# A graph-network and feed-forward kernel on one core: finer waits in the edge trees, roots issued sooner, group 0's rows merged tile by tile, and the sums of chunks 38, 40 and 42 moved to TensorE

## The chip, the cores and the metric

The kernel is one program on one core of a Trainium2 chip. A core has TensorE (PE, matrix products into PSUM), VectorE (DVE), ScalarE (ACT), GpSimd (POOL) and SyncE (SP), each with its own queue of instructions, and 16 DMA engines that all queues share. Engines wait for each other through semaphores. The metric is the device time of one execution in microseconds (us); 0.2% of it is 2.4 us.

## The reference

6250 nodes with 256 features, 200,000 edges with 96 features, sorted by destination `dst`. What the change touches is the first part of the layer:

```python
xn = layernorm(x)
out1 = segment_sum(edge_attr, dst, 6250)
cnt  = segment_sum(1, dst, 6250)
out2 = where(cnt > 0, segment_max(edge_attr, dst, 6250), 0)
out3 = out1 / maximum(cnt, 1)
h    = concat([xn, out1, out2, out3, u])
gnn  = relu(h @ W1 + b1) @ W2 + b2 + xn
mix  = linear_attention(xn)      # q, k squared and normalised, kv, projection
x    = x + gnn + mix
x    = x + ffn(layernorm(x))     # on the half of the nodes with the largest weights
```

## The kernel before

**Edges.** The edges are padded and laid out as 128 partitions of 1568 rows, in 49 chunks of 32 rows per partition. A chunk (1536 KB) is loaded into one of four buffers `xb` by a DMA on SP's queue. Four consecutive rows form a quad, so a chunk has 8 quads. On DVE (`edge_chunk`) a tree first reduces each quad: L995 and L999 take maxima, L998 and L1002 take sums. Then a scan over the 8 quads runs with one step for the maximum (L1018) and one for the sum (L1021) per quad, each from the step before, and writes `ob` (two buffers). SP stores `ob` to `scan_d` in DRAM (a dump, L575), then loads the chunk that is four ahead (L577). Before its first scan step a chunk waits for the dump of the chunk two before it, since it reuses that buffer. For the chunks in `SUMS` the sums of quads come from TensorE instead (`quad_sums`, L1943): four products with the identity for each half chunk, accumulated in one PSUM bank; DVE leaves L998 and L1002 out and its steps L1021 read PSUM. These are chunks 1, 2 and 44 to 48.

**Nodes beside them.** While DVE works through the chunks, TensorE and ScalarE make the projections of 13 groups of 512 nodes (`turn`), with a small normalisation of the keys by DVE after fixed chunks (`NORM`); DVE's key norms of the last two groups come behind chunks 32 and 33. After chunk 35 DVE makes factors (`s_fac`), ScalarE scales the matrix `M` (L1703), and TensorE runs `attention` for the groups (L2122), with ScalarE evicting (L1744), storing each group and fetching the one four ahead on its own DMA queue. In between, the weights of the network are loaded by SP (L596, L599), copied by ScalarE (h0 to h5, L1717) and their low parts made (l0 to l11, L2093) at the groups that `WORK` lists. After chunk 39 DVE computes which rows each node gathers (`rows_to_gather`, ends `s_idx`), after chunk 41 their masks.

**End of the edges.** POOL gathers the raw edge rows of group 0 (`raw0`), ScalarE masks them (L1773 after chunk 46, L1779 after chunk 47). When chunk 48 is done, SP dumps it, and POOL gathers group 0's scan rows (L500), the row to be repaired (L710), group 1's raw rows, writes the repaired row back, gathers group 1's scan rows, then all rows of group 2, and then adds the attention rows to the base rows of group 0 (L756, `bg`). DVE merges group 0's rows for all four tiles at once (`aggregate`, parts 2 to 4) into `agg`; TensorE transposes `agg` (L2168) and begins the hidden layer. The second product of the network (L70, L71) writes PSUM banks psR and psC, and DVE adds `bg` to them (L1182) before the next tile's product may overwrite the bank.

**The rest.** The network over 49 node tiles, the selection of 3124 nodes and the last network follow, with TensorE in the lead.

Of the kernel before, what the change touches and what calls it, by code (L numbers as in the profile page):

```python
# [18 lines left out]
GT = 4  # L19
# [54 lines left out]
def build(nc, x, dstp, edges, u, W1, b1, W2, b2, Wqkv, bqkv, Wout, bout, wr, br, w1, fb1, w2, fb2, out):  # L74
# [10 lines left out]
    with keep:  # L85
# [33 lines left out]
        with ExitStack() as ctx:  # L119
# [331 lines left out]
            psS = {c: psKx if c in SUMS_EARLY else [psR, psC] for c in SUMS}  # L451
# [5 lines left out]
            def weight_piece(i):  # L457
                if i < 8:
# [5 lines left out]
            WORK = {4: ("h0",), 5: ("h1", "l0", "l1"), 6: ("h2", "l2", "l3"), 7: ("h3", "l4", "l5"), 8: ("h4", "l6", "l7"),  # L464
                    9: ("h5", "l8", "l9"), 10: ("l10", "l11")}
# [85 lines left out]
            def _(sp):  # L551
# [18 lines left out]

                def dump_and_load(c, b, load):
# [16 lines left out]
                for c in range(36, CHUNKS):  # L588
# [5 lines left out]
                    if c in (36, 37, 38):  # L594
                        for i in ((0, 1), (2,), (3,))[c - 36]:
                            sp.dma_start(rW1[:, i, :], W1[i * P:(i + 1) * P, :]).then_inc(s_wl[i], 16)  # L596
                    elif c in (39, 40):
# [1760 lines left out]
```

## Time and profile before

| what | value |
|---|---|
| median of 3 runs | 1180.55 us (1180.41 to 1182.44) |
| the profiled execution, its own time | 1180.66 us |
| its span | 1178.9 us |
| PE busy / DVE busy | 1051.5 us (89%) / 991.9 us (84%) |
| ACT busy / POOL busy | 500.4 us (42%) / 451.9 us (38%) |
| mean granted TensorE clock | 0.938 of full |

Busy times are sums over the whole span, which has several stages with different limits; a row of the timeline says what an engine waited for just before an instruction. "DMA share" is the mean busy share of the 16 DMA engines; it can read slightly over 1. A tile name loses its buffer number (`xb` for xb0 to xb3), and names of buffers that share memory are put down by one of them (`W1f_lo`, `rW`, `dprv` as the second query buffer).

### The profile page before, as it was taken

What the parts mean: (1) busy time and instruction counts of PE and PEld (TensorE: products, weight loads), DVE (VectorE), ACT (ScalarE), POOL (GpSimd) and SP (SyncE); (2) the same over time, 40 slices, a digit from 0 to 9 for tenths busy, and PEclk for the clock granted to TensorE, in tenths of its full rate; (3) what the DMA queues carried; (4) which work ended last, traced back from release to release, by engine and by line L of the source; (5) the groups of instructions that cost most, each with busy time, mean ns of one, the idle gap of its engine ahead of it and who ended that gap; (6) DMA issues with size and microseconds to landing.
All of it is one profiled execution on the core that took longest, in us unless ns stands there. A gap on an engine that the chain in (4) does not pass through costs nothing.

```text
span 1178.9 us, 16127 instructions
## 1 busy us (share of the span) xinstructions
PE 1051.5 (89%) x4683; PEld 781.9 (66%) x4683; DVE 991.9 (84%) x2410; ACT 500.4 (42%) x1487; POOL 451.9 (38%) x344
## 2 busy tenths in 40 slices
PE   2598999999988759888999999999999986799996
PEld 1355555656635536466888888888888972488886
DVE  7899999999999997966988889888897757576574
ACT  3547877778832422611332233322333323243341
POOL 0088810888300002076565445654443000223331
PEclk9798999999996979979999999999999996599998
DMA  9799999999988999533443333433333130111110
GB/s 344 288 318 371 346 376 365 356 376 360 335 315 330 415 418 366 189 120 90 133 148 127 123 102 126 150 124 125 107 102 123 54 108 17 38 37 42 46 43 20
DMA packets 76512, 234.99 MB, mean 199 GB/s; under 512 B 13105, under 2 KB 43094, under 8 KB 70178
## 3 DMA queue, kind: packets, MB, share of 16 engines
q1 hardware_dynamic: 42786, 157.00, 35.7%
q0 software_dynamic: 14224, 33.61, 10.0%
q10 hardware_dynamic: 19440, 43.66, 9.9%
q8 instruction: 26, 0.43, 0.2%
q14 instruction: 36, 0.29, 0.1%
HBM read 153.68 MB, written 80.55 MB: 199 GB/s over the span
## 4 chain that ended last, share of the span: by engine, by line
PE 49%; DVE 3%; POOL 2%; issue 1%; DMA 0%; ACT 0%; DVEq 0%; POOLq 0%
PE psR L70 5%; PE psC L70 5%; PE psQ L59 5%; PE psQ L60 5%; PE psKx L59 5%; PE psQ L61 5%; PE psKx L60 5%; PE psKx L61 5%; PE psR L71 3%; PE psC L71 2%; PE psT L2168 1%; PE psQ L2189 1%; PE psKx L2189 1%; POOL graw L474 1%; PE psR L69 1%
## 5 line engine op out<-in xcount | busy, mean ns | idle before, releaser
L474 POOL DMA_INDIRECT graw<-in_edge_attr,ic x90 | 128.7, 1430 | 33.1 <-issue 24.1
L1018 DVE SCALAR_TENSOR_TENSOR ob<-ob,mQ,mx 128x96 f32<-128x96 f32 x392 | 122.3, 312 | 13.4 <-PE psR L1943 6.5
L684 POOL DMA_INDIRECT near<-in_dst,rowi x49 | 87.8, 1792 | 63.8 <-DVEq L924 49.1
L1818 ACT ACTIVATE hT_hi<-psQ 128x512 fp32r<-128x512 f32 (+2 forms) x52 | 29.9, 575 | 186.0 <-PE psQ L2189 142.5
L684 POOL DMA_INDIRECT near<-ends_d,blki x49 | 82.3, 1679 | 68.0 <-DVEq L915 53.4
L1021 DVE SCALAR_TENSOR_TENSOR ob<-ob,kQ,xb 128x96 f32<-128x96 f32 x336 | 104.5, 311 | 0.0
L1970 PE MATMUL psQ<-Wqk,xT 128*128 128x512 f32 (+1 forms) x196 | 94.3, 604 | 0.0
L995 DVE TENSOR_TENSOR mx<-xb 128x1536 f32<-128x1536 f32 x49 | 85.6, 1747 | 1.2 <-DVE carry L1076 0.2
L998 DVE TENSOR_TENSOR xb<-xb 128x1536 f32<-128x1536 f32 x42 | 73.8, 1758 | 1.4
L500 POOL DMA_INDIRECT grow<-scan_d,ic x49 | 54.0, 1101 | 42.8 <-DMA scan_d<-ob 28.1
L70 PE MATMUL psR<-W2w,hT_hi 128*128 128x512 f32 x175 | 65.7, 411 | 3.9 <-DVE x L1184 3.9
L1818 ACT ACTIVATE hT_hi<-psKx 128x512 fp32r<-128x512 f32 (+2 forms) x52 | 29.8, 575 | 88.8 <-PE psKx L2189 88.7
L788 POOL DMA_INDIRECT out_x<-zo,lst x25 | 24.6, 986 | 104.7 <-DVE zo L1474 104.7
L70 PE MATMUL psC<-W2w,hT_hi 128*128 128x512 f32 x168 | 60.8, 399 | 0.0
L1991 PE MATMUL psKx<-xn,kc 128*128 128x257 f32 (+1 forms) x196 | 52.3, 390 | 5.2 <-ACT kc L1594 5.2
L480 POOL DMA_INDIRECT yg<-yrow_d,lst x25 | 24.9, 997 | 82.0 <-DVE lst L1426 74.7
L746 POOL COPY ic<-idx 128x12 int32 (+3 forms) x11 | 4.5, 407 | 134.5 <-PE psC L69 134.5
L1970 PEld LDWEIGHTS psQ<-Wqk,xT 128*128 128x128 f32 (+1 forms) x196 | 38.0, 194 | 26.9 <-issue 24.3
L1982 PE MATMUL psC<-WvoI,xT 128*128 128x256 f32 (+1 forms) x196 | 50.6, 381 | 0.0
L71 PE MATMUL psR<-W2w,hT_lo 128*128 128x256 f32 x175 | 49.9, 285 | 0.0
L71 PE MATMUL psC<-W2w,hT_lo 128*128 128x256 f32 x168 | 47.4, 282 | 0.0
L1174 DVE SCALAR_TENSOR_TENSOR hT_lo<-psQ,hT_hi 128x512 fp32r<-128x512 f32 (+2 forms) x52 | 34.0, 654 | 15.3 <-ACT hT_hi L1818 15.3
(533 smaller groups left out, 3284.4 us busy)
## 6 DMA issues: line engine op xcount, KB each, us to landing
xb<-in_edge_attr SPq DMA_DIRECT2D x49, 1536.0 KB
scan_d<-ob SPq DMA_DIRECT2D x49, 768.0 KB
yrow_d<-yr SPq DMA_DIRECT2D x48, 132.0 KB
xg<-in_x ACTq DMA_DIRECT2D x12, 512.0 KB
xT_d<-xT ACTq DMA_DIRECT2D x12, 512.0 KB
base_d<-dcur ACTq DMA_DIRECT2D x12, 512.0 KB
qT_d<-qT ACTq DMA_DIRECT2D x12, 512.0 KB
out_x<-xres SPq DMA_DIRECT2D x48, 128.0 KB
```

The costliest lines, as they stand in the source:

```text
L59: nc.tensor.matmul(out, lh, rh, start=start, stop=False)
L60: nc.tensor.matmul(out, lh, rl, start=False, stop=False)
L61: return nc.tensor.matmul(out, ll, rh, start=False, stop=stop)
L70: nc.tensor.matmul(out, lh, both.rearrange("p h n -> p (h n)"), start=start, stop=False)
L71: return nc.tensor.matmul(out[:, 0:NF], ll, both[:, 0, :], start=False, stop=False)
L474: nc.gpsimd.indirect_dma_start(out=to.rearrange("p i f -> p (i f)"), out_offset=None, in_=raw_v, in_offset=bass.IndirectOffsetOnAxis(ap=ic ...
L684: nc.gpsimd.indirect_dma_start(out=near[:, t, :], out_offset=None, in_=table, in_offset=bass.IndirectOffsetOnAxis(ap=rows[:, t:t + 1], axi ...
L995: nc.vector.tensor_tensor(mx[:, :, :, :], xp[:, :, :, 0, :], xp[:, :, :, 1, :], ALU.max).then_inc(s_tree, 1)
L998: nc.vector.tensor_tensor(xp[:, :, :, 0, :], xp[:, :, :, 0, :], xp[:, :, :, 1, :], ALU.add).then_inc(s_tree, 1)
L1018: nc.vector.scalar_tensor_tensor(o[:, q, 0:EF], prev[:, 0:EF], mQ[:, bass.ds(c * TQ + q, 1)], mx[:, q, 0, :], ALU.min, ALU.max).then_inc(s ...
L1021: nc.vector.scalar_tensor_tensor(o[:, q, EF:AGG], prev[:, EF:AGG], kQ[:, bass.ds(c * TQ + q, 1)], quad_sum, ALU.mult, ALU.add).then_inc(s_ ...
L1970: ins = nc.tensor.matmul(o, xT[:, c, t * P:t * P + rows], Wqk[:, c, :], start=False, stop=(c == KF - 1))
```

## The change

Seven edits. (1) In a chunk whose sums stay on DVE, the first sum L998 no longer waits for the first maximum, the first scan step waits only for the second maximum, and the second sum is waited for by the first sum step. (2) ScalarE issues the square root of the variances ahead of two small DMAs. (3) TensorE's sums of chunk 2 are split: one half goes to psR and ahead of the node groups, the other behind the first tile of group 0. (4) Chunks 38, 40 and 42 join the ones summed on TensorE; their sums are issued behind the attention of groups 3, 6, 9, that of 44 behind 10, that of 45 behind 11. `WORK` moves h4 to h5 and l8 to l11 by one or two groups, SP loads the weights a chunk earlier, and `rows_to_gather` comes after chunk 38. (5) The last dump goes out in two halves. (6) Five loads for the node stage move from ScalarE's queue to SP's, behind the gathers of group 0's scan rows; POOL makes its constants ahead of those gathers. (7) Group 0's rows are merged tile by tile in `first_rows`, with the parts that don't need the scan rows made beforehand.

```diff
-SUMS_LATE = (44, 45, 46, 47, 48)
+SUMS_LATE = (38, 40, 42, 44, 45, 46, 47, 48)
...
-            WORK = {..., 8: ("h4", "l6", "l7"), 9: ("h5", "l8", "l9"), 10: ("l10", "l11")}
+            WORK = {..., 8: ("l6", "l7"), 10: ("h4", "l8", "l9"), 11: ("h5", "l10", "l11")}
...
+                def last_dump():
+                    c, o = CHUNKS - 1, ob[(CHUNKS - 1) % OB]
+                    for h in range(2):
+                        sp.wait_ge(s_sum, c * TQ + 4 * h + 5)
+                        sp.wait_ge(s_max, c * TQ + 4 * h + 5)
+                        sp.dma_start(scan_v[:, bass.ds(c * TQ + 4 * h, 4), :], o[:, 4 * h:4 * h + 4, :]).then_inc(s_dump[c % OB], 16)
...
+                last_dump()
+                sp.wait_ge(s_at, 6 + KF + 12 * GT)
...
+                for t in range(GT):
+                    sp.wait_ge(s_g0[t], 48)
+                sp.dma_start(xTr[1][:, :, :], ...).then_inc(s_ld[1], 16)
...
                     nc.vector.tensor_tensor(mx[:, :, :, :], xp[:, :, :, 0, :], xp[:, :, :, 1, :], ALU.max).then_inc(s_tree, 1)
+                    if not on_pe:
+                        dve.wait_ge(s_tree, n0)
+                        nc.vector.tensor_tensor(xp[:, :, :, 0, :], xp[:, :, :, 0, :], xp[:, :, :, 1, :], ALU.add).then_inc(s_tree, 1)
                     dve.wait_ge(s_tree, n0 + 1)
-                    if not on_pe:
-                        nc.vector.tensor_tensor(xp[:, :, :, 0, :], xp[:, :, :, 0, :], xp[:, :, :, 1, :], ALU.add).then_inc(s_tree, 1)
...
-                    dve.wait_ge(s_tree, n0 + (2 if on_pe else 4))
+                    dve.wait_ge(s_tree, n0 + (2 if on_pe else 3))
...
+                        if q == 0 and not on_pe:
+                            dve.wait_ge(s_tree, n0 + 4)
...
-                    if c == 39:
+                    if c == 38:
                         rows_to_gather()
...
+                    def first_rows():
+                        each = rcnt[:, 0:GT].rearrange("p (t o) -> p t o", o=1).broadcast_to([P, GT, EF])
+                        step(nc.vector.tensor_tensor(graw[0][:, :, 1, :], graw[0][:, :, 1, :], graw[0][:, :, 2, :], ALU.add), False)
+                        step(nc.vector.tensor_tensor(kept[:, :, 0, :], kept[:, :, 0, :], kept[:, :, 1, :], ALU.max))
+                        step(nc.vector.tensor_tensor(graw[0][:, :, 2, :], graw[0][:, :, 1, :], each, ALU.mult))
+                        for t in range(GT):
+                            dve.wait_ge(s_g0[t], 48)
+                            sums, mean_ = grow[0][:, t, EF:AGG], graw[0][:, t, 2, :]
+                            nc.vector.tensor_tensor(agg[:, t, EF:2 * EF], kept[:, t, 0, :], grow[0][:, t, 0:EF], ALU.max).then_inc(s_lead, 1)
+                            nc.vector.tensor_tensor(agg[:, t, 0:EF], graw[0][:, t, 1, :], sums, ALU.add).then_inc(s_lead, 1)
+                            nc.vector.scalar_tensor_tensor(agg[:, t, 2 * EF:3 * EF], sums, rcnt[:, t:t + 1], mean_, ALU.mult, ALU.add).then_inc(s_lead, 1)
...
-                    for m in range(4):
+                    for m in range(3):
                         hidden_nodes(0, m)
-                    transposes(0, range(GT))
+                    transposes(0, range(2))
+                    hidden_nodes(0, 3)
+                    transposes(0, range(2, GT))
...
-                act.wait_ge(s_ln, 1)
-                nc.scalar.sqrt(sd[:, :], va[:, :]).then_inc(s_sqrt, 1)
-
                 act.wait_ge(s_ln, 2)
...
+                QUADS_BEHIND = {3: 38, 6: 40, 9: 42, 10: 44}
                 for g in range(GROUPS):
                     attention(g, g % 4, g // 4 * 16 + 16)
...
-                    if g == 10:
-                        quad_sums(SUMS_LATE[0])
+                    if g in QUADS_BEHIND:
+                        quad_sums(QUADS_BEHIND[g])
                     weights(g)
+                quad_sums(45)
```

DVE's queue at chunk 37 before (mx_54 and xb_49 are this chunk's maxima and edges, ob_55 and ob_56 the two scan buffers; in brackets the semaphores an instruction waits for):

```order
L995 TENSOR_TENSOR mx_54<-xb_49 128x1536 [waits s_v,s_load1]
L998 TENSOR_TENSOR xb_49<-xb_49 128x16x96 [waits s_tree]
L999 TENSOR_TENSOR mx_54<-mx_54 128x8x96
L1002 TENSOR_TENSOR xb_49<-xb_49 128x8x96 [waits s_tree]
L1018 SCALAR_TENSOR_TENSOR ob_56<-ob_55,mQ,mx_54 128x96 [waits s_max,s_tree,s_dump1]
L1021 SCALAR_TENSOR_TENSOR ob_56<-ob_55,kQ,xb_49 128x96 [waits s_sum]
```

and now:

```order
L1023 TENSOR_TENSOR mx_54<-xb_49 128x1536 [waits s_v,s_load1]
L1026 TENSOR_TENSOR xb_49<-xb_49 128x16x96 [waits s_tree]
L1028 TENSOR_TENSOR mx_54<-mx_54 128x8x96 [waits s_tree]
L1031 TENSOR_TENSOR xb_49<-xb_49 128x8x96 [waits s_tree]
L1047 SCALAR_TENSOR_TENSOR ob_56<-ob_55,mQ,mx_54 128x96 [waits s_max,s_tree,s_dump1]
L1052 SCALAR_TENSOR_TENSOR ob_56<-ob_55,kQ,xb_49 128x96 [waits s_sum,s_tree]
```

The instructions and their order are the same. What each wait is for has changed: the first sum now waits only for the chunk before, the second maximum for the first one, the first maximum step for the second maximum alone, and the first sum step for the second sum.

TensorE's queue from the attention of group 9 on, before (psT<-M is the attention of one group, xb_52 the sums of chunk 44, rW and W2w low parts of weights):

```order
L2122 MATMUL psT<-M,dprv 128x256 x8
L2093 MATMUL psQ<-rW_153,ident 128x512
L2094 MATMUL psQ<-W2w,minus 128x512
L2093 MATMUL psQ<-rW_153,ident 128x512
L2094 MATMUL psQ<-W2w,minus 128x512
L2122 MATMUL psT<-M,xT 128x256 x8
L1943 MATMUL psR<-xb_52,ident 128x384 x4
L1943 MATMUL psC<-xb_52,ident 128x384 x4
```

and now (xb_50 is chunk 42, xb_52 chunk 44):

```order
L2185 MATMUL psT<-M,dprv 128x256 x8
L2000 MATMUL psR<-xb_50,ident 128x384 x4
L2000 MATMUL psC<-xb_50,ident 128x384 x4
L2185 MATMUL psT<-M,xT 128x256 x8
L2000 MATMUL psR<-xb_52,ident 128x384 x4
L2000 MATMUL psC<-xb_52,ident 128x384 x4
L2156 MATMUL psQ<-rW_153,ident 128x512
L2157 MATMUL psQ<-W2w,minus 128x512
```

The sums of chunk 42 stand between the attentions of groups 9 and 10, and l8 and l9 have moved behind the sums of chunk 44.

POOL's queue from the raw rows of group 0 on, before (grow are scan rows, graw raw rows, fix the repaired row):

```order
L474 DMA raw_179<-in_edge_attr,ic 128x384 x8
L500 DMA grow_171<-scan_d,ic 128x192 x4
L710 DMA fix<-scan_d,fixi 128x192
L474 DMA graw_166<-in_edge_attr,ic 128x384 x8
L720 DMA scan_d<-fix,fixi 50305x192
L725 IOTA numi 128x15
L726 IOTA ri 128x512
L728 MEMSET tri 128x128
L730 AFFINE_SELECT tri<-tri 128x128
L500 DMA grow_172<-scan_d,ic 128x192 x4
```

and now:

```order
L475 DMA raw_179<-in_edge_attr,ic 128x384 x8
L730 IOTA numi 128x15
L731 IOTA ri 128x512
L733 MEMSET tri 128x128
L735 AFFINE_SELECT tri<-tri 128x128
L743 DMA grow_171<-scan_d,ic 128x192 x4
L746 DMA fix<-scan_d,fixi 128x192
L475 DMA graw_166<-in_edge_attr,ic 128x384 x8
L757 DMA scan_d<-fix,fixi 50305x192
L501 DMA grow_172<-scan_d,ic 128x192 x4
```

The four constants have moved ahead of group 0's scan rows; all else keeps its order.

## Rows read from the trace of the kernel before

**Rows 1.** Windows: length, busy per engine (count), TensorE clock, DMA share, GB/s.

```profile
140.00:170.00 30.00, 27.69 (x115) 16.76 (x114) 29.59 (x65) 24.56 (x100) 11.88 (x9) 1.00 1.01 369
...
410.00:430.00 20.00, 16.82 (x55) 11.40 (x54) 19.60 (x55) 6.30 (x12) 1.32 (x1) 0.87 1.02 417
...
545.00:967.00 422.00, 418.64 (x2119) 354.64 (x2120) 354.94 (x836) 131.90 (x297) 183.16 (x135) 1.00 0.35 114
```

**Rows 2.** Chain that ended last, at 545 us: start, duration, what.

```profile
545.04 2.37 POOL bg L756
```

**Rows 3.** VectorE timeline, chunk 41: start, us, line, operation, [idle before <- releaser].

```profile
418.57 1.75 DVE L995 TENSOR_TENSOR mx<-xb 128x1536 f32<-128x1536 f32 x1
420.36 1.76 DVE L998 TENSOR_TENSOR xb<-xb 128x1536 f32<-128x1536 f32 x1
422.04 0.95 DVE L999 TENSOR_TENSOR mx<-mx 128x768 f32<-128x768 f32 x1
422.91 0.95 DVE L1002 TENSOR_TENSOR xb<-xb 128x768 f32<-128x768 f32 x1
423.95 0.32 DVE L1018 SCALAR_TENSOR_TENSOR ob<-ob,mQ,mx 128x96 f32<-128x96 f32 x1
...
427.62 0.20 DVE L960 TENSOR_TENSOR a<-Eend,Sbeg 128x49 f32<-128x49 f32 x1
```

**Rows 4.** Timeline of ScalarE at the start.

```profile
45.75 1.28 ACT L1555 ACT_TABLE_LOAD   x1 [2.03 <-DVEq L867]
```

**Rows 5.** Timeline of TensorE at the start.

```profile
54.23 8.30 PE L1943 MATMUL psKx<-xb,ident 128*128 128x384 f32 x16 [7.76 <-DVE ob L1021]
62.37 0.60 PE L1956 MATMUL psT<-ident,xn 128*128 128x128 f32 x4
```

**Rows 6.** Timeline of ScalarE, end of the node projections.

```profile
349.48 0.51 ACT L1593 ACTIVATE kc<-k,rk 106x256 f32<-106x256 f32 x1 [5.97 <-DVE rk L1030]
...
369.84 0.84 ACT L1703 ACTIVATE M<-psQ,kcol 128x256 f32<-128x256 f32 x2 [4.89 <-DVEq L1065]
```

**Rows 7.** Timeline of VectorE, starts of chunks 38, 44, 45, wait, end.

```profile
388.58 1.75 DVE L995 TENSOR_TENSOR mx<-xb 128x1536 f32<-128x1536 f32 x1
...
450.95 1.75 DVE L995 TENSOR_TENSOR mx<-xb 128x1536 f32<-128x1536 f32 x1
...
457.95 1.75 DVE L995 TENSOR_TENSOR mx<-xb 128x1536 f32<-128x1536 f32 x1
...
467.17 0.32 DVE L1018 SCALAR_TENSOR_TENSOR ob<-ob,mQ,mx 128x96 f32<-128x96 f32 x1 [6.47 <-PE psR L1943]
...
492.94 0.29 DVE L1085 COPY cT<-psC 96x128 f32<-96x128 f32 x1 [0.58 <-PE psC L2144]
```

**Rows 8.** Timeline of TensorE, attention of groups 3, 9, sums of 44.

```profile
386.51 1.99 PE L2122 MATMUL psT<-M,kc 128*128 128x256 f32 x8 [0.27 <-ACT xa L1744]
...
440.82 3.78 PE L2122 MATMUL psT<-M,dprv 128*128 128x256 f32 x8 [14.01 <-ACT k L1744]
...
453.34 2.74 PE L1943 MATMUL psC<-xb,ident 128*128 128x384 f32 x8
```

**Rows 9.** Waits over the span: total us, times, longest.

```profile
ACT W2w L1717 <- DMA rW<-in_L_gnn_W: 15.0, 1, 15.0
```

**Rows 10.** DMA issues between 400 and 412 us: KB, us to landing.

```profile
rW<-in_L_gnn_W SPq DMA_DIRECT2D x1, 512.0 KB, 22.7
```

**Rows 11.** Timeline of GpSimd, first gather of scan rows.

```profile
498.80 0.95 POOL L500 DMA_INDIRECT grow<-scan_d,ic  x1 [28.07 <-DMA scan_d<-ob]
```

**Rows 12.** Timeline of ScalarE, masked rows of group 0.

```profile
479.61 4.62 ACT L1773 ACTIVATE graw<-raw,kSel 128x96 f32<-128x96 f32 x17
...
485.99 8.69 ACT L1779 ACTIVATE kept<-raw,unkept,kSel 128x96 f32<-128x96 f32 x24
```

**Rows 13.** Timeline of TensorE, group 0: first hidden product, tile 2's output.

```profile
515.33 0.77 PE L59 MATMUL psQ<-aggT_hi,W1f_hi 128*128 128x512 f32 x1 [1.49 <-DVE tailT L1160]
...
548.36 0.80 PE L70 MATMUL psR<-W2w,hT_hi 128*128 128x512 f32 x1 [3.92 <-DVE x L1184]
```

More of the change, by code:

```diff
@@ L450, in build @@
             psW = psQ + psKx
-            psS = {c: psKx if c in SUMS_EARLY else [psR, psC] for c in SUMS}
+            psS = {c: [psR, psC] for c in SUMS_LATE}
+            psS[SUMS_EARLY[0]], psS[SUMS_EARLY[1]] = psKx, [psR, psKx[0]]
             psA, psH, psO = psT, psQ + psKx, [psR, psC]
@@ L587, in _ @@
                         dump_and_load(g * XB + b, b, True)
-                for c in range(36, CHUNKS):
+                for c in range(36, CHUNKS - 1):
                     dump_and_load(c, c % XB, c + XB < CHUNKS)
@@ L1076, in _ @@
                         step(nc.vector.memset(carry[:, 2 * EF:2 * EF + 1], 1.0))
+                        step(nc.vector.tensor_tensor(unkept[:, :, 5], unkept[:, :, 5], has[:, 0:GT], ALU.mult))
                         dve.sem_inc(s_lead, 1)
@@ L1124, in aggregate @@
                         elif part == 3:
-                            if isinstance(g, int) and g <= 1:
-                                dve.wait_ge(s_g0s, (g + 1) * 16 * GT)
+                            if isinstance(g, int) and g == 1:
+                                dve.wait_ge(s_g0s, 16 * GT)
                             dve.wait_ge(s_am, am0 + 2)
@@ L1267, in node_stage @@
                     aggregate(0, 0, 0, 2)
+                    dve.wait_ge(s_am, 2)
+                    dve.wait_ge(s_as, 2)
+                    step(nc.vector.tensor_tensor(kept[:, :, 1, :], kept[:, :, 1, :], kept[:, :, 2, :], ALU.max), False)
+                    step(nc.vector.tensor_tensor(graw[0][:, :, 2, :], graw[0][:, :, 2, :], graw[0][:, :, 3, :], ALU.add))
                     carries()
-                    for part in range(3, 5):
-                        aggregate(0, 0, 0, part)
+                    first_rows()
+                    for t in range(2):
+                        aggregates_low(0, t)
                     repair()
+                    for t in range(2, GT):
+                        aggregates_low(0, t)
                     dve.wait_ge(s_wlo, LOWS + 4)
@@ L1274, in node_stage @@
                     dve.wait_ge(s_u, 1)
-                    for t in range(GT):
-                        aggregates_low(0, t)
                     selection_constants()
@@ L2017, in turn @@
                         base(g, t)
+                        if g == 0 and t == 0:
+                            quad_half(SUMS_EARLY[1], 1)
                         if t + 2 < nt:
@@ L2029, in _ @@
                 pe.wait_ge(s_wrb, 3)
-                for c in SUMS_EARLY:
-                    quad_sums(c)
+                quad_sums(SUMS_EARLY[0])
+                quad_half(SUMS_EARLY[1], 0)
                 pe.wait_ge(s_wq, 1)
@@ L2136, in _ @@
                 nc.tensor.matmul(psT[0][:, :], ones[:, :], endrow[:, :], start=True, stop=True).then_inc(s_t, 1)
-                for i in range(4):
-                    quad_sums(SUMS_LATE[1 + i])
+                for i in range(3):
+                    quad_sums(46 + i)
                     tail_part(i)
+                tail_part(3)
                 pe.wait_ge(s_max, CHUNKS * TQ + 1)
@@ L2159, in transposes @@
                         for t in tiles:
-                            if t == 0:
+                            if isinstance(g, int) and g == 0:
+                                pe.wait_ge(s_lead, 2 + 5 * (t + 1))
+                            elif t == 0:
                                 pe.wait_ge(s_am, g * NAM + NAM)
```

95 lines of the change are left out of this document (60 added, 35 removed).

## The prediction

> **What bounds the kernel now.** I read the busy time by windows first. Between 140 and 170 us VectorE is busy 29.59 of 30.00 us, and the 16 DMA engines show a share of 1.01 at 369 GB/s; between 410 and 430 us the share is 1.02 at 417 GB/s, TensorE at 16.82 of 20 us. From 545 us on TensorE is busy 418.64 of 422 us at full clock and DMA falls to 0.35 [rows 1]. So the chunks are set by VectorE with the DMA engines close beside it, and the network by TensorE. Second, the chain that ended last runs through POOL's `bg` at 545.04 [rows 2], one DVE addition and TensorE's psR product at 548.36, which had stood 3.92 us for it [rows 13]. Behind it nothing changes. What the change is worth is therefore how much sooner that addition comes. Third, VectorE's timeline in a chunk: from 418.57 to 427.62, 9.05 us for one whose sums stay on DVE [rows 3], and 7.00 us for chunk 44 with sums on TensorE (450.95 to 457.95) [rows 7]. Fourth, POOL's timeline: its first gather of scan rows starts at 498.80 after an idle time of 28.07 us that the last dump ends [rows 11]. From there to the end of `bg`, 547.41, POOL has 48.6 us of gathers and additions which keep their order (only the four constants leave them, and they lie in a wait for the repaired row's store). The end moves as that gather moves, as long as nothing overtakes POOL.
>
> **The roots.** ScalarE waits until 43.72 and loads its table at 45.75, so two DMA issues take 2.03 us ahead of the root [rows 4], and DVE waits for the root before it can start its statistics and chunks. Gain 2.0 us; the two DMAs, now later, feed TensorE's node work, which has slack.
>
> **The finer waits.** Start to start before: first maximum to first sum 1.79 us on a duration of 1.75 (a wait), first sum to second maximum 1.68 on 1.76 (none), second maximum to second sum 0.87 on 0.95 (none), second sum to first scan step 1.04 on 0.95 (a wait) [rows 3]. So a wait for the instruction just ahead costs 0.11 and 0.17 us. After the change neither the first sum nor the second maximum nor the second sum nor the first scan step waits for the one just ahead; what they wait for is one instruction further back. Now 1.68 + 1.68 + 0.87 + 0.87 = 5.10 against 5.38: 0.28 us, and I take 0.30 since the last pair may overlap a little more. This holds for 34 chunks of the first 36 (1 and 2 are summed on TensorE) and for 36, 37, 39, 41, 43: 39 × 0.30 = 11.7 us. Bounds: 0, if waits aren't what opens the gap, and 39 × 0.34 = 13.
>
> By the Trainium skill, page "VectorE: DVE Perf Modes", section "The DRAIN you can't avoid", a VectorE instruction starts only once the pipe behind the one before is empty, "the semaphore costs nothing extra here", and taking waits away gains nothing. By that the term would be 0. The trace [rows 3] speaks against it, with 1.68 on 1.76 where there is no wait and 1.79 on 1.75 where there is one; its time is a rival below.
>
> **Chunks 38, 40 and 42.** Such a chunk loses both sums. From its first maximum to the second it waits (1.79), from the second to the scan too (1.04): 2.83 in place of 5.38, so 9.05 becomes 6.50; chunk 44's 7.00 contains short waits for its sums. Against the 8.75 of the new tree that is 2.25 each, 6.75 us in all. For it TensorE must be in time. Half a chunk's sums take 2.74 us at full clock [rows 8], the whole 5.5. They are queued behind the attention of groups 3, 6 and 9. Attention is tied to `M`, which before started at 369.84 after a wait of 4.89 for DVE [rows 6]; DVE being 2.0 + 34 × 0.30 = 12.2 us earlier, `M` comes at 357.6. Group 3 ended at 388.50 [rows 8], 18.7 after it, so now at 376.3. DVE starts chunk 38 at 388.58 − 12.2 − 0.6 = 375.8 [rows 7] and wants its first half at 378.6; it is there at 379.0 and the second at 381.8, some 2 scan steps late: 0.7 us. For chunk 40 the same counting gives 0.7 again. Behind group 9 the attention, sped up by nothing and delayed by 5.5 for each chunk's sums, comes closest: I take 2.5. Sum of the lateness 3.9 us, bounds 1 and 10. Net gain 2.8.
>
> **The wait at chunk 45.** There DVE stood 6.47 us for sums [rows 7], since TensorE had stood 14.01 us before the attention of group 9 (440.82) for ScalarE [rows 8], which stood 15.0 us for the raw weights `rW` [rows 9], a load that needed 22.7 us from issue to landing [rows 10]. The change puts that copy two groups later and its load a chunk earlier, which covers the 15.0 with 22.1: two groups of attention at 3.8, 5.5 of sums, and the 9.05 of a chunk. The wait goes: 6.5. What is late next is the sums of 46 to 48, behind l8 to l11 now; I count 0.7 of small waits. Net 5.8.
>
> **Transfers.** From chunk 36 to the load of chunk 48 some 39.6 MB have to move by the sizes of the buffers (loads of 1.57 MB and dumps of 0.79 for each chunk, attention groups fetched and stored at 0.52 each, weights at 0.52 a piece [rows 10]), which at 417 GB/s [rows 1] are 95 us. Forecast is a stage of 89 to 100 us, so DMA comes level with DVE and a dump can hold a first scan step. I take 1.1 us lost, bounds 0 and 10.
>
> Sum for the end of chunk 48 (492.4, just ahead of [rows 7]'s 492.94 with its 0.58 wait): −2.0 −11.7 −2.8 −5.8 +1.1 = −21.2.
>
> **The last dump.** From the scan's end at 492.36 to the gather at 498.80 pass 6.4 us [rows 7, 11]. With the first half (4 of 8 quads) sent some 2 us earlier, and without ScalarE's five loads beside it, the second half of half the bytes lands sooner; I take 4.7, so −1.7. Bounds 0 (a small transfer costs mainly its latency) and −3. The loads, behind group 0's gathers, then come some 29 us before TensorE needs them and stay hidden.
>
> **Node groups sooner.** TensorE summed chunk 2 for 8.30 us ahead of the groups, starting 54.23 after a wait of 7.76, and their first transposes came at 62.37 [rows 5]. Half the sums go behind: the groups start near 51.6, but a half is put between. This is slack: at the end ScalarE waits 5.97 for DVE's key norm [rows 6], so the projections are bound by DVE's chunks 32 and 33 and gain only as they do. Worth 0; if the moved half were late, a chunk would stand up to 4 us.
>
> **Group 0's merge.** DVE's parts ahead of the scan rows, then three instructions per tile. TensorE's first product of them came at 515.33, and 29.1 us later, at 548.36 − 3.92 = 544.4, it was ready for the psR that waits for `bg` [rows 13]. Its hidden layer would now start near 515.3 − 22.9, or a little over 1 us sooner by the tiles, say 491 to 493, and be ready at 520 to 522; `bg` ends at 547.41 − 22.9 = 524.5. So the merge by tiles is worth 0 for the end. The cover: ScalarE's masked rows (479.61, then 485.99 to 494.68 [rows 12]) must be there; they hang on the raw gather and on TensorE's and DVE's chunks 46 and 47, and move 16 us to near 478, DVE standing some 4 us for them while the dump and gather run. Against that the cover is 2.5 to 4 us, no more.
>
> **The sum.** −21.2 − 1.7 = −22.9. The profiled execution took 1180.66 us, 0.01% off the median of 1180.55, so 1157.8, which I round to 1158.
>
> **Rivals.** *A, the forecast*: 1158, by its own bounds 1153 to 1163. *B, waits cost nothing*, the pipe between two instructions being what opens the gap (for it: the gap of the pairs without a wait is nearly as long; against it: 1.68 is shorter than the 1.76 it follows): all else stays, −22.9 + 11.7 = −11.2, 1169. *C, the DMA engines hold the chunks*: their share is at 1 in both windows; if 369 GB/s is what the first stage can draw, DVE merely waits for loads where it now saves 0.30, and 34 × 0.30 = 10.2 is lost: 1168; with the late stage alone held, 95 + 10 us, also 1168. For it: the share. Against it: 417 GB/s was moved at the same share, while 9.05 us going to 8.75 asks 369 × 9.05 / 8.75 = 382. *D, group 0 ends last*: TensorE or ScalarE's masks pass POOL by 2 to 4 us, 1160 to 1162. *E, slower*: ScalarE's wait for `rW` comes back at h4 or one of its neighbours before group 9, with TensorE's sums of chunk 42 now queued behind that attention. Before, 14.01 us there cost DVE 6.47, since chunk 44 was the first to need it; chunks 42 and 44 now need it 18 us earlier. From an attention of group 9 at 441 or later (forecast 419) the standing of DVE eats up the 22.9, and 4 us of lateness in the rest give 1184. Against it: the copies are ordered after group 10. *F, the edits don't do what they say*: the waits and orders of the queues show that they do; I give it nothing.
>
> By the Trainium skill, page "DMA: Bandwidth & Descriptors", section "Specifications", one core has about 358 GB/s of the chip's memory and 435 GB/s as the ceiling of its fabric. The 417 GB/s of [rows 1] are above the first and near the second; were the first the limit, C would be the case.
>
> **How the numbers follow.** A 0.62, D 0.09, B 0.10, C 0.14, E 0.05. The range takes all of A and D and reaches to B and C, whose centres are 1168 and 1169: 1152 to 1169. A measurement of this kernel tells 0.2%, 2.4 us, from no change. A to D lie over 9 us below 1178, so faster has 0.94; E is slower, 0.04 of its 0.05, and same has 0.02.
>
> **What would show it.** In the changed profile: first maximum to first sum 1.68 and chunks of 8.75 us (B if 9.05 stays; C if DVE waits for `xb` loads in front of them); `M` near 357.6; no wait over 1 us for psR or psC in chunks 38 and 40, at most 3 in 42 and none of 6 in 45; TensorE's attention of group 9 near 419 (E if after 441); POOL's first gather of scan rows near 476 and 4.7 us after the scan's end; `bg` near 522 to 524 and still last in the chain before psR (D if DVE adds later than that for another releaser). I am wrong if TensorE's network stage behind it takes more than its 418.64 of 422 us, since nothing in it is meant to change.

## The result and the profile after

The changed kernel took 1219.31 us (median of 4 runs, 1213.37 to 1221.78) against 1181.21 before: ratio 1.0314, 95% interval 1.0271 to 1.0358. It is 38 us slower; 1158 was forecast. The profiled execution, the fastest of the four, has a span of 1211.6 us against 1178.9.

The loss sits in two stretches of the first stage, the two in which GpSimd gathers. These are windows of the changed kernel: one in each of the two, and one between them (length, busy time and count of PE, PEld, DVE, ACT and POOL, TensorE clock, DMA share, GB/s):

```profile
110.00:140.00 30.00, 11.05 (x38) 7.06 (x39) 16.67 (x42) 10.73 (x45) 25.43 (x16) 0.67 0.74 247
200.00:230.00 30.00, 29.22 (x117) 17.71 (x115) 24.12 (x57) 22.02 (x82) 4.99 (x4) 1.00 0.89 345
290.00:320.00 30.00, 15.05 (x57) 8.81 (x56) 14.93 (x39) 10.72 (x38) 25.19 (x16) 0.77 0.72 260
```

Where [rows 1] had VectorE at 29.59 of 30 us, it has 16.67 and 14.93 here, and the DMA share is no longer 1 but 0.74 and 0.72: neither VectorE nor the DMA engines lead. The list of waits (total, times, longest, in us) says who waited for whom:

```profile
DVE rk L1059 <- ACT junk L1666: 51.9, 6, 22.2
ACT jc L1572 <- DMA near<-ends_d,blki: 27.5, 3, 17.9
ACT jc L1581 <- DMA near<-in_dst,rowi: 24.6, 2, 16.1
```

VectorE stood 51.9 us before its key norms for ScalarE; in the profile before no such wait is listed. ScalarE stood 27.5 and 24.6 us for `near`, rows that GpSimd gathers in two rounds of 49 (L705) and that ScalarE counts between the node groups. The waits chain up, here at the end of chunk 9 (start, duration, what, idle time before and who ended it):

```profile
97.63 1.63 POOL L705 DMA_INDIRECT near<-ends_d,blki  x1 [0.30 <-issue]
99.57 1.36 POOL L705 DMA_INDIRECT near<-ends_d,blki  x1 [0.30 <-issue]
101.24 1.44 POOL L705 DMA_INDIRECT near<-ends_d,blki  x1 [0.30 <-issue]
102.98 8.44 POOL L705 DMA_INDIRECT near<-ends_d,blki  x1 [0.30 <-issue]
111.72 8.44 POOL L705 DMA_INDIRECT near<-ends_d,blki  x1 [0.30 <-issue]
120.46 3.36 POOL L705 DMA_INDIRECT near<-ends_d,blki  x1 [0.30 <-issue]
...
133.58 0.34 ACT L1572 ACTIVATE jc<-near,nhalf 128x56 bf16<-128x56 int32 x1 [17.92 <-DMA near<-ends_d,blki]
...
139.20 1.42 PE L2067 MATMUL psT<-ident,q 128*128 128x128 f32 x4 [18.09 <-ACT qT L1707]
...
136.31 0.17 DVE L1059 TENSOR_SCALAR rk<-k2s 128x4 f32<-128x4 f32 x1 [13.30 <-ACT junk L1666]
```

Two gathers in a row take 8.44 us each, and their starts lie 8.74 us apart, the length of one chunk. Then ScalarE waits 17.92 us for the batch, TensorE 18.09 for ScalarE's copy, VectorE 13.30 for the squares of the keys. While VectorE stands, from 124 to 136 us, each gather takes 0.94 or 0.95 us. TensorE comes back slowly: its granted clock is 0.50, the lower level, from 136 to 145 us, and the four products of the row above take 1.42 us against 0.60 at 89.59; what this adds to the loss was not followed. GpSimd's timeline of before, in chunks 5 and 6, reads:

```profile
90.48 3.89 POOL L684 DMA_INDIRECT near<-ends_d,blki  x1 [0.30 <-issue]
94.68 1.49 POOL L684 DMA_INDIRECT near<-ends_d,blki  x1 [0.30 <-issue]
96.47 1.43 POOL L684 DMA_INDIRECT near<-ends_d,blki  x1 [0.30 <-issue]
98.21 1.03 POOL L684 DMA_INDIRECT near<-ends_d,blki  x1 [0.30 <-issue]
```

The longest there is 3.89 us. From the first start to the last end, 49 gathers took 96.9 and 102.5 us before and 138.9 and 135.8 now, though the first starts sooner, at 55.5 against 57.4. What has changed beside them is VectorE's tree:

```profile
105.44 1.75 DVE L1023 TENSOR_TENSOR mx<-xb 128x1536 f32<-128x1536 f32 x1
107.11 1.75 DVE L1026 TENSOR_TENSOR xb<-xb 128x1536 f32<-128x1536 f32 x1
108.78 0.95 DVE L1028 TENSOR_TENSOR mx<-mx 128x768 f32<-128x768 f32 x1
109.64 0.95 DVE L1031 TENSOR_TENSOR xb<-xb 128x768 f32<-128x768 f32 x1
110.51 0.31 DVE L1047 SCALAR_TENSOR_TENSOR ob<-ob,mQ,mx 128x96 f32<-128x96 f32 x1
...
114.18 1.75 DVE L1023 TENSOR_TENSOR mx<-xb 128x1536 f32<-128x1536 f32 x1
```

Start to start 1.67, 1.67, 0.86, 0.87 and 8.74 us for the chunk: the spacing that was forecast, to 0.01 us. In this chunk's rows no moment is left in which VectorE stands idle between instructions. The gather that starts at 102.98 ends at 111.42, 0.9 us after the first scan step starts (110.51), though no idle moment lies there. The long one of before started at 90.48 and ended at 94.37, 0.8 us after VectorE's idle moment ahead of the first sum (93.59).

By stretches, against the profile before, with two of the experiments (e1 has the old waits in the trees, e9 the finer ones and no gathers; both below). Each is a difference of two rows of VectorE or GpSimd; minus is sooner. The sum is for the profiled executions, whose own times differ by 32.7 us; the medians differ by 38.

| stretch (us before) | forecast | changed | e1 | e9 |
|---|---|---|---|---|
| to the start of chunk 36 (369.9) | -12.2 | +39.4 | -3.3 | -12.7 |
| chunk 36 to the last scan step (122.5) | -9.0 | -6.1 | -7.3 | -3.0 |
| last scan step to the first scan-row gather (6.4) | -1.7 | -3.2 | -3.2 | -1.1 |
| that gather to the first addition of `bg` (48.6) | 0 | +3.2 | +3.5 | +3.2 |
| sum | -22.9 | +33.4 | -10.2 | -13.5 |

The first row of the changed kernel is VectorE's 51.9 us of waits less the 12.7 us that e9 gains there. Behind the last row the changed kernel takes 630.8 us to the end of its span, against 631.5 before: nothing was lost there.

### The profile page after: what moved, and what is told of

It reads as the page before. It is cut to its first block, busy times and chain, and to the rows that moved or that the text cites. A ratio compares the mean times of both kernels' runs of the same rounds, so it can differ in the third digit from the quotient of the medians.

```text
span 1211.6 us, 16303 instructions
## 1 busy us (share of the span) xinstructions
PE 1067.0 (88%) x4731; PEld 791.0 (65%) x4731; DVE 980.0 (81%) x2420; ACT 501.3 (41%) x1487; POOL 531.2 (44%) x344
## 4 chain that ended last, share of the span: by engine, by line
PE 48%; DVE 3%; POOL 1%; issue 1%; DMA 0%; ACT 0%; DVEq 0%; POOLq 0%
PE psR L70 5%; PE psC L70 5%; PE psQ L59 5%; PE psQ L60 4%; PE psQ L61 4%; PE psKx L59 4%; PE psKx L60 4%; PE psKx L61 4%; PE psR L71 3%; PE psC L71 2%; PE psT L2236 1%; PE psQ L2257 1%; PE psKx L2257 1%; POOL graw L475 1%; PE psR L69 1%
## 5 line engine op out<-in xcount | busy, mean ns | idle before, releaser
L705 POOL DMA_INDIRECT near<-ends_d,blki x49 | 124.2, 2536 | 66.1 <-DVEq L943 51.5
L705 POOL DMA_INDIRECT near<-in_dst,rowi x49 | 121.2, 2473 | 44.3 <-DVEq L952 29.7
L1047 DVE SCALAR_TENSOR_TENSOR ob<-ob,mQ,mx 128x96 f32<-128x96 f32 x392 | 122.5, 313 | 11.5 <-PE psR L2000 5.4
L1052 DVE SCALAR_TENSOR_TENSOR ob<-ob,kQ,xb 128x96 f32<-128x96 f32 x312 | 97.4, 312 | 0.0
L816 POOL DMA_INDIRECT out_x<-zo,lst x25 | 24.6, 984 | 104.0 <-DVE zo L1531 104.0
L1026 DVE TENSOR_TENSOR xb<-xb 128x1536 f32<-128x1536 f32 x39 | 68.3, 1752 | 0.0
L2067 PE MATMUL psT<-ident,q 128*128 128x128 f32 (+1 forms) x98 | 19.1, 304 | 46.1 <-ACT qT L1707 45.7
L2052 PE MATMUL psKx<-xn,kc 128*128 128x257 f32 (+1 forms) x196 | 55.7, 410 | 0.4 <-ACT kc L1650 0.4
L2067 PEld LDWEIGHTS psT<-ident,q 128*128 128x128 f32 (+1 forms) x98 | 10.8, 148 | 58.8 <-issue 55.9
## 6 DMA issues: line engine op xcount, KB each, us to landing
xb<-in_edge_attr SPq DMA_DIRECT2D x49, 1536.0 KB, 10.2
```

What stands on the lines that cost most here:

```text
L705: nc.gpsimd.indirect_dma_start(out=near[:, t, :], out_offset=None, in_=table, in_offset=bass.IndirectOffsetOnAxis(ap=rows[:, t:t + 1], axi ...
L1026: nc.vector.tensor_tensor(xp[:, :, :, 0, :], xp[:, :, :, 0, :], xp[:, :, :, 1, :], ALU.add).then_inc(s_tree, 1)
L1047: nc.vector.scalar_tensor_tensor(o[:, q, 0:EF], prev[:, 0:EF], mQ[:, bass.ds(c * TQ + q, 1)], mx[:, q, 0, :], ALU.min, ALU.max).then_inc(s ...
L1052: nc.vector.scalar_tensor_tensor(o[:, q, EF:AGG], prev[:, EF:AGG], kQ[:, bass.ds(c * TQ + q, 1)], quad_sum, ALU.mult, ALU.add).then_inc(s_ ...
```

## The experiments

**e1, e2: which edit.** e1 is the changed kernel with the old waits (first sum behind `n0 + 1`, scan behind `n0 + 4`). e2 is the kernel before with edit 1 alone:

```diff
-                    dve.wait_ge(s_tree, n0 + 1)
                     if not on_pe:
+                        dve.wait_ge(s_tree, n0)
                         nc.vector.tensor_tensor(xp[:, :, :, 0, :], ..., ALU.add).then_inc(s_tree, 1)
+                    dve.wait_ge(s_tree, n0 + 1)
```

> The changed kernel with the old waits in the trees of VectorE (edit 1 undone, all else as changed). Theory P: GpSimd's gathers of near get through only where VectorE stands still for a moment, and the old waits are such moments; with them back the 49 gathers of a round take about 97 us as before (139 us in the changed kernel), ScalarE does not wait for near, VectorE has no wait of over 1 us at a key norm, and the time is 1171 to 1177 (before, less 2.0 for the roots, less 4.6 in chunks 36 to 48, the rest as it came out). Theory N: the node groups, which now start 10 us sooner, run ahead of the gathers whatever the waits; VectorE's waits at the key norms stay at 30 us or more and the time at 1200 or more.

> The kernel before with edit 1 alone (finer waits in all chunks). Theory P: the gathers of near slow to about 2.8 us each, ScalarE waits for them and VectorE for ScalarE, 25 to 50 us in all at the key norms, so 1195 to 1220. Theory N: gathers as before, no waits at the key norms, 1180.6 - 11.7 = 1169.

e1: 1170.15 us, ratio 0.9913 (0.9898 to 0.9929). e2: 1223.91 us, ratio 1.0362 (1.0344 to 1.0379). One edit holds the whole loss, and the other six together gain 10 us. Both times lie outside what was expected, e1 by 1 us below it and e2 by 4 us above it, and e2's wait of 52.6 us is above the 25 to 50 expected; which theory holds does not hang on that. In e1 the two rounds take 99.8 and 102.5 us, the longest gather 3.89; in e2 138.9 and 133.4, the longest 8.45. The waits of e2:

```profile
DVE rk L1031 <- ACT junk L1613: 52.6, 4, 27.1
ACT jc L1527 <- DMA near<-in_dst,rowi: 27.2, 2, 21.0
ACT jc L1518 <- DMA near<-ends_d,blki: 22.1, 3, 17.4
```

Its node groups start no sooner than before (TensorE's first transposes at 63.43 us against 62.37 in [rows 5]), so theory N (the groups run ahead of the gathers) falls.

**e3: the waits by chunk.**

```diff
-dve.wait_ge(s_tree, n0)
+dve.wait_ge(s_tree, n0 + (1 if (1 < c < 14 or 17 < c < 30) else 0))
-dve.wait_ge(s_tree, n0 + (2 if on_pe else 3))
+dve.wait_ge(s_tree, n0 + (2 if on_pe else 4 if (1 < c < 14 or 17 < c < 30) else 3))
```

> The changed kernel with the old waits in chunks 3 to 13 and 18 to 29, where GpSimd gathers, and the finer ones in the other 16. Theory P: gathers as before, no waits at the key norms, 16 x 0.30 = 4.8 us gained on the run with old waits everywhere: 1166 to 1172. Theory N: 1200 or more.

1168.65 us (1166.84 to 1174.40), 0.9903 (0.9882 to 0.9924): inside the forecast, and 1.5 us below e1, which the intervals don't separate. Chunk 36 starts 1.1 us sooner than in e1, and chunks 36 to 48 take 2.1 us longer; VectorE waits 7.4 us in three places there for dumps, against 5.2 in e1. It also waits 2.1 us once at a key norm, where none was expected. So the finer waits in the 16 other chunks have no gain clear of the noise: the 4.8 us expected of them did not come.

**e4, e5: one idle moment or the other.** e4 keeps the old wait ahead of the first sum only, e5 the one ahead of the scan only.

> The changed kernel with only the wait ahead of the first sum back as it was, the one ahead of the scan left finer. In the trace of before long gathers (3.89 us) end 0.8 us after the idle moment ahead of the first sum. Theory P1: that moment alone lets a gather through; gathers take some 2.0 us on the mean, 1165 to 1172. Theory P2: each of the two moments lets one through; with one of them the gathers take 2.3 to 2.6 us each and VectorE still waits 5 to 30 us at the key norms, 1175 to 1200. Theory N: as the changed kernel.

> The counterpart of e4_first_wait_kept: only the wait ahead of the first scan step back as it was, the one ahead of the first sum left finer. If each of the two idle moments lets a gather through and they weigh alike: the 49 gathers of a round take 115 to 125 us, the longest 5 to 6 us, VectorE waits 10 to 30 us at the key norms, 1180 to 1195. If only the first moment matters (theory P1, which e4 weakened): gathers as in the changed kernel, 139 us for 49, longest 8.44, 1210 to 1220. If only this one matters: 97 to 100 us for 49, about 1170.

**e6: an idle moment elsewhere.** The changed kernel with one wait more, in the middle of the scan:

```diff
+                        if q == 4 and not on_pe:
+                            dve.wait_ge(s_sum, c * TQ + q + 1)
                         dve.wait_ge(s_max, c * TQ + q + 1)
```

> The changed kernel, fine waits in the trees as they are, with one wait more for each chunk summed on VectorE: in the middle of its scan a step waits for the step just ahead. It adds some 0.1 us to a chunk, 39 of them 4 us. Theory P (idle moments of VectorE let the gathers through): a wait more makes the kernel faster; the longest gathers fall from 8.44 to 5 to 7.5 us, 49 of them take 115 to 130 us, VectorE's waits at the key norms fall from 52 to 10 to 35 us, 1185 to 1205. Theory Q (it is the order of reads and writes within the tree that holds the gathers, a wait elsewhere does nothing): gathers unchanged, 1219 + 4 = 1223.

The times, and GpSimd's gathers of each, from the profiled execution (the first round from its first start to its last end, the longest of both rounds, us):

| kernel | waits on the instruction just ahead, per chunk | 49 gathers | longest | VectorE's wait at key norms | time |
|---|---|---|---|---|---|
| before | first sum, scan | 96.9 | 3.89 | 0 | 1181.21 |
| e1 | first sum, scan | 99.8 | 3.89 | 0 | 1170.15 |
| e4 | first sum | 119.0 | 5.04 | 18.6 | 1185.25, ratio 1.0040 (1.0027 to 1.0053) |
| e5 | scan | 125.6 | 7.30 | 30.0 | 1199.55, ratio 1.0146 (1.0123 to 1.0168) |
| e6 | middle of the scan | 114.0 | 5.46 | 0 | 1174.41, ratio 0.9940 (0.9915 to 0.9966) |
| changed | none | 138.9 | 8.44 | 51.9 | 1219.31 |

e4 is where P2 put it; e5 lies above its range and 14 us above e4, so the moment ahead of the scan is worth less than the one ahead of the first sum. Each idle moment shortens the gathers, whichever instruction makes it, so P1 (the first alone) and Q (the order within the tree) fall. e6 is the sharpest: it does more waiting than the changed kernel and is 45 us faster. I had expected 1185 or more; the size was off because 114 us was already soon enough for ScalarE, so that no key norm waited in the profiled execution. That was the fastest of its six, which spread from 1166.56 to 1178.06; whether the slower ones waited is not shown. GpSimd's timeline in e6:

```profile
104.63 1.53 POOL L705 DMA_INDIRECT near<-ends_d,blki  x1 [0.31 <-issue]
106.46 0.97 POOL L705 DMA_INDIRECT near<-ends_d,blki  x1 [0.30 <-issue]
107.73 5.46 POOL L705 DMA_INDIRECT near<-ends_d,blki  x1 [0.30 <-issue]
113.50 1.52 POOL L705 DMA_INDIRECT near<-ends_d,blki  x1 [0.30 <-issue]
...
105.02 0.32 DVE L1054 SCALAR_TENSOR_TENSOR ob<-ob,kQ,xb 128x96 f32<-128x96 f32 x1
105.38 0.32 DVE L1049 SCALAR_TENSOR_TENSOR ob<-ob,mQ,mx 128x96 f32<-128x96 f32 x1
```

VectorE pauses between 105.02 and 105.38 (0.36 start to start, 0.23 elsewhere in the scan); the gather under way ends 0.8 us later (106.16), the next takes 0.97, and the one that starts with the next tree is held for 5.46.

**e7: the price of edit 4.** e1 with only chunks 44 to 48 summed late on TensorE, and `WORK`, the loads and `rows_to_gather` as before:

```diff
-SUMS_LATE = (38, 40, 42, 44, 45, 46, 47, 48)
+SUMS_LATE = (44, 45, 46, 47, 48)
...
-                QUADS_BEHIND = {3: 38, 6: 40, 9: 42, 10: 44}
+                QUADS_BEHIND = {10: 44}
```

> The kernel of e1_old_waits with edit 4 undone: only chunks 44 to 48 summed on TensorE in the late stage, with the weights, loads and rows_to_gather where they stood before. It prices edit 4. The forecast had 2.8 + 5.8 us for it: then 1178 to 1180 here, 8 over e1's 1170.15. If transfers hold the late stage either way (chunk 36 to the end of 48 took 114.9 us in e1 against 122.5 before), less: 1172 to 1177. If the 6.47 us wait at chunk 45 comes back whole, a run of over 6 us of VectorE's idle time before psR shows there.

1179.51 us (12 runs), 0.9987 (0.9970 to 1.0004). Edit 4 is worth 9.4 us on e1, where the forecast had 2.8 + 5.8 = 8.6. ScalarE's wait for `rW`, 17.2 us, is back with it, and so is VectorE's at chunk 45, 6.48 us.

**e9, e12: without the gathers.** One memset of `near` and raised semaphores take the place of the 98 gathers, in the changed kernel (e9) and in the kernel before (e12), so that segment ends and what hangs on them are not computed rightly:

```diff
-                    for t in range(TILES):
-                        nc.gpsimd.indirect_dma_start(out=near[:, t, :], ...).then_inc(s_near[t // BATCH], 16)
+                    for i in range(BATCH):
+                        pool.sem_inc(s_near[i], 16 * BATCH)
```

> The changed kernel, finer waits everywhere, without GpSimd's 98 gathers of near: one memset fills near once and the semaphores are raised, so the nodes' segments and what hangs on them are not computed rightly; ScalarE, TensorE and VectorE do all their work. Theory P (the finer waits cost only through the gathers): no wait of over 1 us at a key norm, the 50 us are gone and the finer waits bring at last what they save. How much of the 11.7 us: theory A (VectorE's chunks lead up to M): M at 355 to 359, 1157 to 1161. Theory R (TensorE's projections, busy 30.00 of 30 us between 200 and 230, lead): VectorE waits at key norms for a few us in all or M for TensorE, M at 361 to 366, 1163 to 1168. If P is wrong, 1200 or more.

> The kernel before without the 98 gathers of near (as in e9, so segments are not computed rightly): the control for e9. VectorE's chunks led there and the gathers were done in time, so 1178 to 1181. If their transfers or their hold on VectorE cost the chunks time, less: 1170 to 1177, and then part of what e9 gains on e1 is not the finer waits' doing.

e12: 1180.88 us, 0.9999 (0.9982 to 1.0017); the gathers cost the kernel before nothing that can be measured. e9: 1165.31 us, 0.9870 (0.9838 to 0.9903). With the gathers, the finer waits put the changed kernel 49 us above e1; without them it is 4.8 us below e1. Chunk 36 starts at 357.16 and ScalarE's `M` at 357.10, where 357.6 was forecast. The time lies in the range of theory R (TensorE's projections lead) and above that of A, but `M` comes where A had it, so R falls as the reason. Of the 9.4 us by which the profile misses the forecast, 6.0 lie between chunk 36 and the last scan step and 3.2 in GpSimd's chain behind it (the table). The first show on VectorE, with the window of that time:

```profile
400.96 0.32 DVE L1047 SCALAR_TENSOR_TENSOR ob<-ob,mQ,mx 128x96 f32<-128x96 f32 x1 [4.92 <-DMA scan_d<-ob]
...
414.06 0.32 DVE L1047 SCALAR_TENSOR_TENSOR ob<-ob,mQ,mx 128x96 f32<-128x96 f32 x1 [4.30 <-DMA scan_d<-ob]
...
450.85 0.32 DVE L1047 SCALAR_TENSOR_TENSOR ob<-ob,mQ,mx 128x96 f32<-128x96 f32 x1 [3.23 <-PE psR L2000]
```

```profile
395.00:415.00 20.00, 20.00 (x75) 13.48 (x74) 10.74 (x27) 9.87 (x18) 0.00 (x0) 1.00 1.03 422
```

VectorE is busy 10.74 of 20 us and waits 4.92 and 4.30 us for dumps, while the DMA share is 1.03 at 422 GB/s: in this stretch, chunks 40 and 41, the transfers lead, and what VectorE brings is partly given back. Its third row is a wait for TensorE's sums, at chunk 45.

**e8, e10, e11: the end of the edges.** In the changed kernel and in e1, GpSimd's chain from the first scan-row gather to `bg` is 3 us longer than before, against a forecast of none. The changed kernel, on ScalarE's, VectorE's and GpSimd's timelines:

```profile
513.25 0.58 ACT L1785 CAST W1t<-psQ 98x512 fp32r<-98x512 f32 x1 [9.56 <-DMA att_d<-yr]
...
526.48 8.69 ACT L1835 ACTIVATE kept<-raw,unkept,kSel 128x96 f32<-128x96 f32 x24
...
535.40 1.36 DVE L1152 TENSOR_TENSOR kept<-kept 128x1152 f32<-128x1152 f32 x1 [4.62 <-ACT kept L1835]
536.67 1.35 DVE L1155 TENSOR_TENSOR graw<-graw 128x1152 f32<-128x1152 f32 x1
...
528.96 2.20 POOL L743 DMA_INDIRECT grow<-scan_d,ic  x1 [22.94 <-DMA scan_d<-ob]
...
538.30 1.22 POOL L475 DMA_INDIRECT graw<-in_edge_attr,ic  x1 [2.13 <-DVE graw L1155]
```

ScalarE's last masked rows end at 535.2, 9.4 us after the last scan step (525.7), because it stood 9.56 us for a store and then 4.83 for TensorE before it began them; VectorE waits 4.62 for them, GpSimd 2.13 for VectorE. e8 puts the first 24 masked rows of e1 ahead of the second `tail_rows`. e10 also puts VectorE's `nodes_low` of group 1 behind the additions of group 0. e11 has both on top of e3.

```diff
-                for i in range(2):
-                    tail_rows(i)
-                act.wait_ge(s_ld[0], 16)
-                nc.scalar.copy(xTs[0][:, :, :], xTr[0][:, :, :]).then_inc(s_xh, 1)
+                tail_rows(0)
                 def masked_rows():
...
+                    tail_rows(1)
+                    act.wait_ge(s_ld[0], 16)
+                    nc.scalar.copy(xTs[0][:, :, :], xTr[0][:, :, :]).then_inc(s_xh, 1)
                     act.wait_ge(s_sum, 48 * TQ + 1)
```

> The kernel of e1_old_waits with ScalarE's first 24 masked rows of group 0 ahead of the copy of the second piece of W1t and of the group's node columns, so that it does not wait for TensorE between. In e1 ScalarE ends the masked rows 9.5 us after the last scan step, VectorE waits 4.63 us for them, and GpSimd's gather of group 1's raw rows waits 2.13 us for VectorE; from the first gather of scan rows to VectorE's addition of bg 52.2 us pass against 48.6 before. If that is the cause of the 3.5 us: masks end some 5 us sooner, the 2.13 us wait and most of the 3.5 us go, 1166.5 to 1168. If not: 1170.

> The kernel of e8_masks_sooner, with VectorE's subtraction for the node columns of group 1 (xTs_lo) behind the additions of group 0 instead of ahead of them. In e8 that subtraction stood beside GpSimd's addition of bg and took 5.54 us, 1.2 us elsewhere, and the first addition to x came at 539.88 with bg ready at 536.4. If the two engines hold each other up there: the first addition follows bg within 0.3 us, 49 to 50 us after the first gather of scan rows, and the time is 1166.5 to 1168. If the slow subtraction had another cause or its place is needed by TensorE: 1170 to 1171.

> Both edits of e10 on top of e3_waits_by_chunk (finer waits in the 16 chunks without gathers). e3 took 1168.65; with the 3 us of e10, if it comes, 1165 to 1167, the best of all. If e10 brings nothing 1168 to 1169.

e8: 1170.78 us, 0.9912 (0.9897 to 0.9927), no gain on e1. `bg` is ready 49.6 us after the first gather, as meant. But see VectorE and GpSimd there, and the same subtraction in e1:

```profile
534.31 5.54 DVE L1200 TENSOR_TENSOR xTs_lo<-xTr,xTs_hi 128x1024 fp32r<-128x1024 f32 x1
539.88 0.42 DVE L1214 TENSOR_TENSOR x<-bg,psR 128x256 f32<-128x256 f32 x1
...
534.03 4.73 POOL L784 TENSOR_TENSOR bg<-bg,tg 128x1024 f32<-128x1024 f32 x2
```

```profile
529.02 1.23 DVE L1200 TENSOR_TENSOR xTs_lo<-xTr,xTs_hi 128x1024 fp32r<-128x1024 f32 x1
537.22 0.42 DVE L1214 TENSOR_TENSOR x<-bg,psR 128x256 f32<-128x256 f32 x1 [6.98 <-POOL bg L784]
```

The subtraction that takes 1.23 us in e1, where GpSimd is gathering, takes 5.54 beside GpSimd's two additions, and ends 1 us after them: here GpSimd holds VectorE. So the first addition comes 53.1 us after the first gather, against 52.2 in e1, and the 1168 or less that was expected did not come. e10: 1174.45 us, 0.9937 (0.9913 to 0.9961). The first addition to `x` comes at 536.47, as soon as `bg` is there and 49.9 us after the gather, so the two did hold each other up. The time still went up by 4 us on e1, above both ranges expected. From the first addition to the end, the profile of e10 is 4.6 us longer than that of e1; TensorE's wait of 2.63 us for the moved subtraction, at 548.34, is one part, and what takes the rest was not followed. e11: 1171.24 us, 0.9913 (0.9892 to 0.9935), above both ranges expected too. Neither beats e3, which has the lowest median of the versions that compute everything; the intervals of e1, e3, e8 and e11 overlap.

## Why the prediction was wrong

**The failed step** is "The finer waits": 39 × 0.30 = 11.7 us, with the bound of 0 on the bad side. The gain itself is real and about right in size: 8.74 us for a chunk in place of 9.05, and 12.7 us to chunk 36 in e9 against 3.3 in e1, so 9.4 us for 34 chunks where 10.2 was counted. But it showed only where the gathers were left out. The bound was wrong: I priced what the edit does to VectorE and not what VectorE's idle moments did for another engine. GpSimd's gathers of `near` stand in no row and no rival of the prediction. In the profile before, POOL (the fifth engine of a windows row) was busy 26.04 of 30 us with them, and one kind of gather took 1.03 us at one time and 3.89 at another: a sign that something held them.

```profile
110.00:140.00 30.00, 28.83 (x116) 18.13 (x115) 29.56 (x66) 24.53 (x100) 26.04 (x14) 1.00 1.01 359
```

In place of a gain, gathers beside gapless chunks take up to 8.44 us, a round takes up to 139 us, and the batches come too late for ScalarE; shown by e1 to e6 and e9.

The Trainium skill speaks of it, page "SBUF — State Buffer", section "Who interferes with whom": GpSimd and VectorE share a pair of ports, taken by one of them for a whole instruction, and a VectorE instruction with two SBUF inputs contends with a GpSimd instruction that reads SBUF. The trees and scans have two such inputs, and e8 shows VectorE held by GpSimd. But by that rule a wait would last for one instruction (1.75 us at most for a gather), and the traces show several: 8.44 us for a gather, and in e8 both of GpSimd's additions.

A break in VectorE's instructions is not GpSimd's only way in. In the changed kernel's chunk 7 (96.72 to 105.44), which has no break, the gathers that start at 97.63, 99.57 and 101.24 take 1.63, 1.36 and 1.44 us, and each ends 0.9 us after a step of the tree or the first scan step starts. The one that starts at 102.98, during the scan, gets past none of the scan steps and tree steps that follow and ends only behind the next chunk's first scan step. So breaks shorten the gathers, as e4 to e6 show; what in the hardware decides when GpSimd is let in, no run shows.

**The rule weighed in the prediction**, the Trainium skill's "The DRAIN you can't avoid" (rival B), is not borne out in the form used there: the trees went from 5.38 to 5.07 us with the same instructions when two waits went. The same section adds that a next instruction which is not held starts earlier, and the rows without a wait show that: 1.67 us from start to start on a duration of 1.75.

**Roots sooner**: forecast 2.0, measured 3.3 in e1. The rest goes with the earlier first half of chunk 2's sums: TensorE's first transposes came at 50.55 (51.6 forecast, 62.37 in [rows 5]), and VectorE's two short waits in chunk 2 (0.54 and 0.77 us before) are gone.

**Chunks 38 to 45**: forecast 8.6, measured 9.4 by e7 against e1. In the changed kernel VectorE waits 2.25 and 0.51 us for the two halves of chunk 38 (0.7 counted) and 0.17 for chunk 40. The wait of [rows 7] at chunk 45 has shrunk from 6.47 us to 1.99, and is not gone; chunk 46 waits 1.15.

**Transfers**: forecast a loss of 1.1 us. In the changed kernel VectorE waits 4.3 us for dumps, in chunks 40, 41 and 44, and the stage took 116.4 us for the 113.5 forecast, though VectorE was late. With VectorE on time (e9) it took 119.5: 6 us too many, with 9.2 us of waits for dumps and 5.1 for sums where 1.1 and 4.6 were counted. That is rival C in its late half. Its early half (the first 34 chunks held by transfers) fell: in e9 VectorE has no wait for a load or dump before chunk 40.

**The last dump**: forecast 1.7, measured 3.2, just past the far bound, in the changed kernel and e1; 1.1 in e9, and why it is less there was not followed.

**Group 0's merge**: forecast 0 at the end, with ScalarE's masked rows done at 478, 7 us after the scan's end. They end 9.4 us after it, and GpSimd's chain grows by 3.2. The step that failed is "POOL's gathers keep their order, so the end moves as the first gather moves": the order was kept, but one gather in it waits for VectorE's merge. It is rival D in size, on POOL's chain and not beside it.

**The slower rival** (E, ScalarE's wait for `rW`) was a mechanism that did not happen: that wait went, as the forecast had it, and came back where edit 4 was undone (e7). The kernel became slower for a reason that no case had.

## What to carry to other kernels

Before a wait is taken out of an engine that is busy 29 of 30 us, look at what shares its resources and is done just in time: an idle moment of 0.1 us can be another engine's turn. The trace of before shows it where the same small instruction takes 0.95 us at one time and 3.89 at another. Where the other engine works in known stretches, the breaks can be kept there and taken out elsewhere (e3); here that gained nothing clear of the noise on keeping them all (e1). One break in another place (e6) gave back most of the loss, with a median 4 us above e1.

## What the runs showed of the hardware

- An indirect gather of 128 rows on GpSimd takes 0.94 us at best, up to 3.89 where VectorE's chunks have two breaks, and up to 8.44 where they have none.
- The other way round, a 128x1024 subtraction on VectorE took 5.54 us beside two GpSimd additions of the same size (e8), and 1.23 in e1, where it ran before them.
- A wait for the VectorE instruction just ahead costs 0.11 us behind one of 1.75 us and 0.17 behind one of 0.95 [rows 3]; without it the next starts 0.08 us before the end of the last.
- A DMA share of 1 is no one rate: 422 GB/s at 1.03 in chunks 40 and 41 of e9, 369 at 1.01 in [rows 1].
